# Local attention in a fused kernel: weights turned in 32x32 blocks on VectorE, value products swapped to 32 rows

## What is computed

```python
def attn_layer(x, Wqkv, qs, ksc, Wo):              # x: (2, 1024, 128)
    q, k, v = jnp.split(x @ Wqkv, 3, -1)           # each (2, 1024, 16 * 64)
    q, k, v = (sh(q), sh(k), sh(v))                # heads apart
    q = l2norm(q) * qs
    k = l2norm(k) * ksc
    q = q * cos * scale + rotate_half(q) * sin * scale
    k = k * cos * inv + rotate_half(k) * sin * inv
    out = local_attention(q, k, v)
    return out @ Wo

def local_attention(q, k, v):                      # windows of w = 32 rows
    bk2, bv2 = look(bk), look(bv)                  # a window and the one before: 64 keys
    sim = jnp.einsum('bhwie,bhwje->bhwij', bq, bk2) * 8.0
    sim = jnp.where(mask, -jnp.finfo(sim.dtype).max, sim)
    attn = jax.nn.softmax(sim, -1)
    out = jnp.einsum('bhwij,bhwje->bhwie', attn, bv2)
    ...

for i in range(6):
    x = attn_layer(shift_tokens(x), Wqkv[i], q_scale[i], k_scale[i], Wo[i]) + x
    x = ffn_layer(shift_tokens(x), ln_g[i], ln_b[i], W1[i], b1[i], W2[i], b2[i]) + x
```

## Time and profile before

| | us |
|---|---|
| median of 3 runs | 4426.52 |
| lowest, highest | 4419.78, 4433.16 |
| the profiled execution | 4439.44 |
| its span, first to last instruction | 4438.1 |
| PE busy / weight loads | 3859.1 / 2706.7 |
| DVE busy | 3062.1 |
| POOL busy | 2649.1 |
| ACT busy | 2568.4 |

### The profile page before, as it was taken

The page is one execution under the profiler, slowest core; times in us unless marked ns, Lnnn a source line. Parts: engine busy times, 40 slices in busy tenths (PEclk is TensorE's granted clock), DMA queues, the critical chain, the costliest instruction groups (busy, mean ns, idle before and its releaser), DMA issues. The chain is left out here.

```text
span 4438.1 us, 158857 instructions
## 1 busy us (share of the span) xinstructions
PE 3859.1 (87%) x66864; PEld 2706.7 (61%) x66864; DVE 3062.1 (69%) x6301; ACT 2568.4 (58%) x4921; POOL 2649.1 (60%) x2218
## 2 busy tenths in 40 slices
PE   7968694399999999999999623999999999999996
PEld 5645453266667666676676422676666676766764
DVE  4446464678777777777777347777777777777773
ACT  3325251266666676666676401666667676666664
POOL 2029074477667676676776203776766767767662
PEclk7569797699999999999999855999999999999998
DMA  0010100133332333333322101333323333233222
GB/s 15 1 33 1 35 1 5 45 93 78 83 85 70 90 80 82 81 82 78 83 65 71 45 7 35 93 82 81 91 65 90 80 85 85 73 87 83 64 71 55
DMA packets 307779, 280.48 MB, mean 63 GB/s; under 512 B 158840, under 2 KB 205696, under 8 KB 307072
## 3 DMA queue, kind: packets, MB, share of 16 engines
q1 hardware_dynamic: 307072, 270.33, 23.9%
HBM read 55.22 MB, written 1.05 MB: 13 GB/s over the span
## 5 line engine op out<-in xcount | busy, mean ns | idle before, releaser
L1459 ACT ACTIVATE m_sq<-PS 128x512 f32<-128x512 f32 x384 | 226.2, 595 | 197.6 <-PE PS L1312 160.8
L1459 ACT ACTIVATE l_sq<-PS 128x512 f32<-128x512 f32 x384 | 226.2, 595 | 196.5 <-PE PS L1312 160.1
L1724 POOL TENSOR_TENSOR l_Pm<-l_Pm,l_rs 128x1024 f32<-128x1024 f32 x96 | 182.9, 1905 | 238.2 <-DVE l_rs L1596 238.2
L1724 POOL TENSOR_TENSOR m_Pm<-m_Pm,m_rs 128x1024 f32<-128x1024 f32 x96 | 182.9, 1905 | 233.7 <-DVE m_rs L1596 233.7
L124 POOL TENSOR_TENSOR rstd<-rstd,minus_half 128x4 f32<-128x4 f32 x40 | 41.9, 1046 | 378.5 <-DVE rstd L120 378.5
L1614 DVE TENSOR_TENSOR XN<-PS,XN 128x128 f32<-128x128 f32 x192 | 56.2, 293 | 279.4 <-PE PS L1364 279.3
L1583 DVE TENSOR_TENSOR l_QR<-PS,l_rot 128x512 f32<-128x512 f32 x192 | 131.8, 687 | 163.2 <-ACT l_sq L1459 163.2
L1583 DVE TENSOR_TENSOR m_QR<-PS,m_rot 128x512 f32<-128x512 f32 x192 | 131.8, 686 | 163.0 <-ACT m_sq L1459 163.0
L1719 POOL TENSOR_TENSOR m_QR<-m_QR,m_UQ 128x1024 f32<-128x1024 f32 x96 | 227.7, 2372 | 24.0 <-DVE m_UQ L1586 24.0
L1719 POOL TENSOR_TENSOR l_QR<-l_QR,l_UQ 128x1024 f32<-128x1024 f32 x96 | 227.7, 2372 | 23.3 <-DVE l_UQ L1586 23.3
L1719 POOL TENSOR_TENSOR l_KR<-l_KR,l_UK 128x1024 f32<-128x1024 f32 x96 | 227.0, 2364 | 0.2 <-DVE l_UK L1586 0.2
(11 more groups left out here) (388 smaller groups left out, 11840.8 us busy)
## 6 DMA issues: line engine op xcount, KB each, us to landing
l_V<-l_Vt SPq DMA_DIRECT2D x576, 128.0 KB
m_V<-m_Vt SPq DMA_DIRECT2D x576, 128.0 KB
l_V<-l_Vt SPq DMA_DIRECT2D x384, 64.0 KB
m_V<-m_Vt SPq DMA_DIRECT2D x384, 64.0 KB
l_wqkv<-l_wqkv_dram SPq DMA_DIRECT2D x72, 128.0 KB, 2.4
m_wqkv<-l_wqkv_dram SPq DMA_DIRECT2D x72, 128.0 KB, 2.5
l_rot<-l_rot_dram SPq DMA_DIRECT2D x24, 256.0 KB, 3.8
m_rot<-l_rot_dram SPq DMA_DIRECT2D x24, 256.0 KB, 3.8
```

The source lines that it names most:

```text
L1459: ac.activation(sq[:, c, b * 512:(b + 1) * 512], PS[:, 2 * c + b, :], ACT.Square).then_inc(sq_out)
L1724: gp.tensor_tensor(pm, pm, over(rs[:, :], 2, [P, 16, 2 * LW]), ALU.mult).then_inc(pn_out)
```

## The change

In the stack, both times:

- DVE transposes Pm in blocks of 32x32 (`turn_weights`, new, at the head of DVE's step). PE's `weights_turn` and ACT's copy `weights_turned` are gone, and so is the buffer pT.
- `values` is written with the roles swapped: V is the stationary side (32 rows by 64 columns), the turned weights Wt move (32 columns). A window's 64 keys are no longer one product but two that add up: one on Vs (V moved down by 32 rows, the window before) and one on Vt (its own). So there are 128 products per tile where there were 64. Window w writes to bank 4+w. The result is O already transposed; `output_turn` on PE is gone, and ACT's two copies of O and two of oT become two that read across four banks.
- V is no longer spread by 10 transfers per tile but moved by two (`shift_v`), into one of two buffers.
- One maximum over both score banks takes the place of two; the rotation's two half-width products become one with swapped halves. Both are on DVE.
- `output` and its addition move from step n+1 to step n+2, just behind `project_q`; on PE `project_v` now comes ahead of `values`. The feed-forward steps move by one to three steps, their turns and "down" use bank 6, and "up" stands behind `turn_q`. The loop has three steps more.

The core of the diff:

```diff
-                    def weights_turn(n):
-                        te.wait_ge(pn_out, n + 1)
-                        at_ge(te, ot_out, 2 * n)
-                        for b in range(2):
-                            to_bank(6 + b, [Pm[:, n % 2, c, :, :].rearrange("p r k -> p (r k)")
-                                            for c in range(4 * b, 4 * b + 4)]).then_inc(w_turn)
-
                     def values(n):
-                        te.wait_ge(v_spread, 160 * (n + 1))
-                        te.wait_ge(wT_out, 2 * n + 2)
+                        te.wait_ge(wT_out, n + 1)
+                        te.wait_ge(V_out, n + 1)
+                        te.wait_ge(v_shift, 32 * (n + 1))
+                        te.wait_ge(ms_out, 2 * min(n + 2, NL))
+                        at_ge(te, y_add, n)
+                        at_ge(te, nT_out, past(n, 7))
+                        at_ge(te, f_add, past(n, 9))
+                        te.wait_ge(XST_out, NG + min(past(n, 10), FG - NG))
                         for c in range(8):
-                            for w in range(4):
-                                for r in range(2):
-                                    m = te.matmul(PS[LW * w:LW * (w + 1), 6 + r, c * LD:(c + 1) * LD],
-                                                  pT[64 * r:64 * r + 64, c, LW * w:LW * (w + 1)],
-                                                  V2[64 * r:64 * r + 64, w, c, :], start=True, stop=True, skip_group_check=True)
+                            for k, V in ((0, Vs), (1, Vt)):
+                                for w in range(4):
+                                    rows = slice(LW * w, LW * (w + 1))
+                                    for r in range(2):
+                                        m = te.matmul(PS[64 * r:64 * r + 64, 4 + w, c * LW:(c + 1) * LW],
+                                                      V[rows, n % 2, r * 512 + c * LD:r * 512 + (c + 1) * LD],
+                                                      Wt[rows, c, r, k, :], start=(k == 0), stop=(k == 1), skip_group_check=True)
                         m.then_inc(val_mm)
...
                     def values_out(n):
                         ac.wait_ge(val_mm, n + 1)
-                        at_ge(ac, ot_turn, 2 * n)
-                        for r in range(2):
-                            ac.copy(O[:, :, r, :], PS[:, 6 + r, :].rearrange("p (c d) -> p c d", d=LD)).then_inc(ov_out)
-
-                    def output_turned(n):
+                        at_ge(ac, out_pr, n)
                         for b in range(2):
-                            ac.wait_ge(ot_turn, 2 * n + b + 1)
-                            at_ge(ac, out_pr, n)
-                            ac.copy(oT[:, 4 * b:4 * b + 4, :].rearrange("p c q -> p (c q)"), PS[:, 6 + b, :]).then_inc(ot_out)
+                            half = slice(4 * b, 4 * b + 4)
+                            ac.copy(oT[:, half, :].rearrange("p c (w i) -> p c w i", w=4),
+                                    PS[:, 4:8, 128 * b:128 * b + 128].rearrange("p w (c i) -> p c w i", i=LW)).then_inc(ot_out)
...
+                    def turn_weights(n):
+                        ve.wait_ge(pn_out, n + 1)
+                        at_ge(ve, val_mm, n)
+                        ve.transpose(Wt[:, :, :, :, :].rearrange("p c r k i -> p (c r k i)"),
+                                     Pm[:, n % 2, :, :, :].rearrange("p c r k -> p (c r k)")).then_inc(wT_out)
...
-                    def spread_v(n):
+                    def shift_v(n):
                         sp.wait_ge(V_out, n + 1)
-                        at_ge(sp, val_mm, n)
...
+                        at_ge(sp, val_mm, n - 1)
+                        sp.dma_start(Vs[LW:P, n % 2, :], Vt[0:P - LW, n % 2, :]).then_inc(v_shift, 16)
+                        sp.dma_start(Vs[0:LW, n % 2, :], Vt[P - LW:P, (n - 1) % 2, :]).then_inc(v_shift, 16)
```

More of the change, by code:

```diff
@@ L1368, in norm_turn4 @@
                         te.wait_ge(xnorm_out, g + 1)
-                        te.wait_ge(ms_out, 2 * min(s + 1, NL))
+                        te.wait_ge(ot_out, 2 * min(s, NL))
                         at_ge(te, f_add, g)
-                        to_bank(4, [xnorm[:, j, :] for j in range(4)]).then_inc(n_turn)
+                        te.wait_ge(XST_out, NG + min(past(s - 1, 10), FG - NG))
+                        to_bank(6, [xnorm[:, j, :] for j in range(4)]).then_inc(n_turn)
                     def up(s, g, c):
@@ L1395, in turn_x @@
                     def turn_x(g):
-                        to_bank(4, [Y[:, 4 * g + j, :] for j in range(4)]).then_inc(x_turn)
+                        to_bank(6, [Y[:, 4 * g + j, :] for j in range(4)]).then_inc(x_turn)
                     for g in range(NG):
@@ L1401, in pe @@
                         turn_x(g)
-                    for s in range(-2, 4 * FG + 8):
-                        widened, narrowed, turned = phase(s, 6), phase(s, 7), phase(s, 8)
-                        if 1 <= s <= NL:
-                            weights_turn(s - 1)
+                    for s in range(-2, 4 * FG + 11):
+                        normed, widened, narrowed, turned = phase(s, 7), phase(s, 8), phase(s, 9), phase(s, 10)
                         if s + 2 < NL:
                             project_q(s + 2)
+                        if 2 <= s <= NL + 1:
+                            output(s - 2)
                         if 0 <= s < NL:
@@ L1416, in pe @@
                         if 1 <= s <= NL:
-                            output_turn(s - 1)
+                            values(s - 1)
+                        if 0 <= s + 1 < NL:
+                            turn_k(s + 1)
+                            turn_q(s + 1)
+                        if normed is not None:
+                            norm_turn4(s, normed)
                         if widened is not None:
-                            norm_turn4(s, widened)
+                            for c in range(3):
+                                up(s, widened, c)
                         if narrowed is not None:
@@ L1550, in act @@
                             turned(s + 1, 0)
+                        if normed is not None:
+                            copy_norm(normed)
                         if widened is not None:
@@ L1556, in act @@
                                 ac.preload_act_table_set("natural_log_exp_and_others")
+                        if xT is not None and xT < FG - NG:
+                            copy_x(xT + NG, xT % NG)
                 def dve():
@@ L1562, in softmax @@
                         at_ge(ve, ms_out, 2 * n)
-                        for r in range(2):
-                            V.step(ve.tensor_reduce(mx[:, r, :], banks[r], AX, ALU.max))
-                        at_ge(ve, w_turn, 2 * (n - 1))
-                        ve.wait_ge(dve_own, V.n - 1)
+                        V.step(ve.tensor_reduce(mx[:, :, :], PS[:, 4:6, :].rearrange("p r (c k) -> p r c k", c=8), AX, ALU.max))
+                        at_ge(ve, wT_out, n - 1)
+                        V.wait()
                         ve.tensor_tensor(Pm[:, n % 2, :, 0, :], banks[0], over(mx[:, 0, :], 2, [P, 8, 2 * LW]), ALU.subtract).then_inc(ms_out)
-                        V.wait()
                         ve.tensor_tensor(Pm[:, n % 2, :, 1, :], banks[1], over(mx[:, 1, :], 2, [P, 8, 2 * LW]), ALU.subtract).then_inc(ms_out)
```

137 lines of the change are left out of this document (47 added, 90 removed).

## The result

The changed kernel takes 5130.18 us (median of four runs, 5128.17 to 5139.40), the kernel before 4423.15 beside it. The ratio is 1.160, with a 95% interval of 1.157 to 1.162. It is slower, as forecast, but by 707 us where 283 were forecast. The time lies above the range of 4580 to 4870.

What follows compares the result with a forecast made beforehand. PE was taken to bound the stack. Per group, products 63.7, ACT wait 4.35 and instruction stops 6.0 make 74.1 us against 68.2, +283 us over 48 groups: 4710 us forecast, range 4580 to 4870.

Steps and rivals of the forecast that it cites:

- PE's products: On PE per step: 256 value passes at 11.0 ns, 2.82 us; two turns of 0.87 go; 63.7 us per group of four steps.
- rival 2: Value passes on PE: two column tiles of a row group take turns, values 5.2 us, time about 4980; chance 8%.
- DVE's block transpose and V's transfers: DVE's new transpose takes 1.23 us and hides; V's two transfers have more than a step; both cost nothing.
- Rival 3: ACT or DVE takes over: copies at 0.8 us, late transpose, +2 us per group, 4800; within the forecast's 84%.
- The stops: In the value run PE waits for late blocks of 256 instructions: 1.5 us per step, 6.0 per group.
- the full stop: In the value run, wait for the next instruction block: 3.7 - 1.41 - 0.35 = 1.9 us, in three of four steps.
- the block that ends early in the run: Block ending in the value run's first fifth or so: nothing waits for it, though the following one may be late.
- the block's turn: When the next instruction block is due; PE was taken to be at least 0.35 us behind it.
- Rival 1: PE's instruction blocks come in time: group 68.1 us, time about 4420, within 35 us; chance 8%.
- The wait for ACT's copies: PE waits for copied k and q: 1.75 us before "up", 1.3 in two steps with turns of four; 4.35 per group.
- The sum: Group 63.7 + 4.35 + 6.0 = 74.1 us against 68.2: +5.9, times 48 groups +283, giving 4710.

## Why the prediction was wrong in size

**PE's products: right.** 256 passes were to take 2.82 us; without their stops they take 2.77 in the median. Sixteen passes start within 0.13 us in the timeline above (1717.08 to 1717.21). The two column tiles of a row group do not take turns, so rival 2 falls. By the 25 ns that the Trainium skill (TensorE: Matmul & The Clock Gate, "Wait — 56ns, not 53.3ns?") gives as the least distance of two starts, the time was estimated at about 5120. The measured time lies there by luck: the median distance of two starts is 8 ns, so the trace does not agree with the 25, and the time comes from stops and clock.

**DVE's block transpose and V's transfers: right.** The transpose takes 1.24 us, as the 1.23 taken from the earlier trace rows, and hides; the values do not wait for V. Rival 3 made no difference: ACT's copies over four banks take 0.59 us each, as the copies of before do.

```profile
L1569 DVE STREAM_TRANSPOSE m_Wt<-m_Pm 128x1024 f32<-128x1024 f32 x96 | 118.7, 1236 | 17.7 <-PE PS L1333 16.7
```

**The stops: right in kind, mis-sized.** The step that failed is "the full stop in three of four steps and 0.1 for the rest: 1.5 us per step". It measured 2.30 us, and no step went without: 175 of 192 runs have one stop and 17 have two, 2.1 us each in the mean where 1.9 was taken. I gave the block that ends early in the run a free pass, and I took PE to be 0.35 us behind the block's turn. The double run with the old products shows the same kind, 2.59. Over 192 steps the difference is 0.80 x 192 = 154 us. Rival 1, blocks in time, is excluded. The Trainium skill (Runtime: NRT & Kernel Launch, "Instruction fetch mechanics") has the crossing of a block's end mostly hidden. Before, the trace agrees (533 packets and 108 stops); after, every one of the 192 runs of the values has at least one stop, so there it does not.

**The clock: missing altogether.** Every duration of the sum came from rows at the upper level, and I never asked what PE's own stops would do to it. The sum had new stops in it, and the earlier trace rows shows both levels of the clock; I did not bring the two together. The kernel before had a warning in its trace. Its stops for instructions are idle times of at most 1.5 us and gave none, but its waits for V's spread, those of the earlier trace rows, are longer: behind each of the five over 2.5 us the clock fell. One of them:

```profile
1790.31 1.93 PE L1334 MATMUL PS<-l_V,l_pT 64*32 64x64 f32 x128 [2.52 <-DMA l_V<-l_Vt]
1792.17 2.86 PE L1318 MATMUL PS<-l_wqkv,XNT 128*128 128x512 f32 x4
```

The v projection takes 2.86 us there and 1.98 in the earlier trace rows. This is the larger miss. Per group the measured 85.3 us (4095 / 48) are 63.7 of products, 9.2 of stops, 1.6 of waits for ACT and 2.7 of the stacks' two ends (the 70.9 of before less 68.2). That leaves 8.1, which is 389 us in all. The table above shows where: the turns of k and q, the turns of four, "up" and "down" take 478 us more; 77 of it is the wait for ACT, and 46 are stops for instructions in the turns (L1266 in the view of waits). The clock accounts for the size: in the 905 us of low clock of the changed kernel PE was at work for some 800, 245 of them in the turn of k and 259 in that of q, and work that takes twice its time loses half of that, some 400 us; before it was 29 of 31 us, a loss of 15. This is an estimate from the starts and the clock of the trace, and with the 46 us beside it the balance is good to some 50 us. That the stops are what lowers the clock is shown in kind by the runs with 60 and 48 waits. Their idle times are longer than those of the changed kernel, and why it falls so readily behind 1.6 to 1.9 us stays open.

**The wait for ACT's copies: too high by 2.75 us per group.** 4.35 were forecast, 77 us / 48 = 1.6 measured. The two turns at half clock last 3.5 us, as long as ACT's three pairs of copies, so the slow clock paid for this wait. With the clock up, in the kernel with half of the products, it is 3.2 per group (155 us) and 1.35 in a step with a turn of four, where 1.3 was forecast. So the forecast was too high by 1.15 at the upper level too.

**The sum.** Stops +154, clock (with the stops in the turns) +389, ACT -132: together +411 on the forecast of 4710, which gives 5121, against 5130. Two of the three errors have the same sign, and the range had no room for a mechanism that was not in the sum.

## What to carry to other kernels

Count instructions in a row, not only their time: a run of 512 short ones costs 2.3 us of stops here where a run of 256 costs 0.2 to 0.3, and the same products placed between slow ones have about a third of the stops. Then take each new stop and ask what the engine's clock does behind it: 1.4 us of idle was nearly free of that in the old kernel, 2.4 and 2.9 us put the next parts at half speed in most steps, and in the changed kernel 1.6 to 1.9 us already did. Look in the trace that you have for the longest waits and at the parts behind them. Before moving a product to cover a wait, look at what else stands in its old place, since it may give another engine its time.

## What the runs showed of the hardware that was not expected

- TensorE's granted clock fell to 1.2 GHz behind most idle times of 2.4 to 2.9 us in otherwise busy stretches (148 of 160 between 2.2 and 2.6 us in the kernel with half of the products and 48 waits), but seldom behind 1.39 (low clock 92 us against 31). The fall may come at once or one part later.
- At the same idle time it fell far more often in the changed kernel (81 of 89 at 1.6 to 1.9 us) than in the old ones (6 of 33). The cause is open.
- A stop for instructions of over 0.3 us nearly always ends 2.2 to 3.2 us after the last packet of the instruction queue began, in all kernels here, and no two packets began closer than 3.25 us. How long the stop is depends on when the packet began, which stays unexplained.
- Short passes on 32 rows by 64 columns start 8 ns apart in the median, 10.8 on average over a run; between such runs of 64 passes a turn of eight tiles takes 1.02 us instead of 0.87.
